# Layer normalisations of a two-layer model: ScalarE makes the high parts, VectorE the full values, on two PSUM banks in turn

## The chip, the cores and the metric

The kernel runs on one core of a Trainium2 chip. The metric is the device time of one execution in microseconds (us); lower is better. Before the change the median of three runs is 2249.2 us (2247.33 to 2249.74).

The engines are named as the profile names them: PE is TensorE's matmul, PEld its weight load, DVE is VectorE, ACT is ScalarE, POOL is GpSimd, SP is SyncE. "L876" is line 876 of the kernel before.

## The reference, cut to what matters

Four batches of 1024 rows with 256 features go through two layers. Each layer has two residual branches, and each branch starts with a layer normalisation that is scaled and shifted per batch:

```python
h = _layernorm(x, axis=-1) * (1 + ca) + sa
x = x + ga * _L0_attn_ref(h, ...)      # gated long convolution
h = _layernorm(x, axis=-1) * (1 + cb) + sb
x = x + gb * _L0_ffn_ref(h, ...)       # FFN with binarised weights, exact GELU
h = _layernorm(x, axis=-1) * (1 + ca) + sa
x = x + ga * _L1_attn_ref(h, ...)      # causal attention, 16 heads on 4 KV heads
h = _layernorm(x, axis=-1) * (1 + cb) + sb
x = x + gb * _L1_ffn_ref(h, ...)       # the two experts chosen per batch
```

## The kernel before, in words

Everything is float32. Where a product needs full precision, an operand is kept as two parts of the reduced type F32R: the high part is the value rounded to that type, the low part is the full value minus the high part. `hT[:, 0]` is the high and `hT[:, 1]` the low part of the transposed, normalised input of a branch. The matmuls that read `hT` (`split_mm` at L300 and `sign_mm` at L306) need both.

One batch is one turn of a hardware loop on every engine; the engines run the same stages and meet by semaphores. In order of time, a batch is: the convolution branch, the FFN, attention, the experts. There are four normalisations in a turn: LN_FFN, LN_ATT, LN_MOE and LN_NEXT (the convolution's, for the next batch). The first batch's own is made once ahead of the loop. Each is made in two halves of 512 rows (h = 0 and 1), and a half goes like this:

1. DVE `normed`: it ends the statistics, hands the variance to POOL, which returns `rstd` (L1140, 1.02 us), and writes four tiles of `hrow` (L867).
2. PE `normed`: for each of two feature tiles dt it transposes four tiles of `hrow` into one PSUM bank (L378).
3. ACT `normed`: for each dt it reads the bank twice with the same scale and bias. L672 writes the full value into `hfull`, L673 the rounded one into `hT[:, 0]`, and that counts `hT_done`.
4. DVE `h_low`: for each dt it waits for `hT_done` and writes `hT[:, 1] = hfull - hT[:, 0]` (L876), which counts `h_lo_done`. PE waits for it in `h_ready`, and ACT waits for it before it writes a ring slot of `hfull` again.

What stands around each half in DVE's program order matters, since each engine works strictly in its order:

- LN_FFN 0: `h_low` stands between `skip_and_gate(1)` and `add_to_x("out0", 1)`; PE makes `long_out(1)` meanwhile, and then the first half of the FFN.
- LN_FFN 1: PE turns it after five of the first half's eight FFN tiles. DVE does `hrow`, then splits four GELU tiles (L1059 and L1061), then `h_low`, then twelve more splits. PE waits for this `h_low` before the second half.
- LN_ATT 0: DVE does `add_to_x("ffn2", 1)` and then `h_low`; then PE projects tiles 0 to 3 (L300).
- LN_ATT 1: DVE does `hrow`, `rotate` of two tiles, `h_low`; then PE projects tiles 4 to 7.
- LN_MOE 0: PE turns it ahead of the last tile of the attention's output product (L610), and the router needs its low part.
- LN_MOE 1: `h_low` stands behind the split of the first expert's weights. Behind it DVE splits the second expert's and makes LN_NEXT's statistics.
- LN_NEXT: `h_low` for both halves stands behind both `hrow`; the next instruction on DVE is the first `add_to_x("moe2", 0)`.

PSUM has eight banks, taken in turn; `bk.take(..., until=...)` names the semaphore count that makes a bank free for PE again.

Of the kernel before, what the change touches and what calls it, by code (L numbers as in the profile page):

```python
# [85 lines left out]
def adaln_hyena_binffn_gqa_moe(nc, d, out, gate_scratch, kf_scratch, scratch):  # L86
    es = ExitStack()
    with es:
# [121 lines left out]
        def rotated(t):  # L210
# [12 lines left out]
                 "rstd_done", "hrow_done", "hT_done", "bias_added", "tap_made", "tap_done", "edge_done", "conv_done", "vx_done",  # L223
# [68 lines left out]
        def _(pe):  # L292
# [77 lines left out]
            def normed(k, h):  # L370

                for dt in range(ND):
                    b = bk.take(pe, ("ln", k, h, dt), until=(s["hT_done"], (k * NHALF + h) * ND + dt + 1))
                    for u in range(4):
                        t = 4 * h + u
                        if dt == 0:
                            pe.wait_ge(s["hrow_done"], k * NT + t + 1)
                        i = tr(ps[:, b, u * P:(u + 1) * P], hrow[:, t, dt * P:(dt + 1) * P], ident[:, :])  # L378
                    i.then_inc(ready[b], 1)
# [260 lines left out]
        def _(act):  # L640
# [23 lines left out]
            def normed(k, h, mod):  # L664

                for dt in range(ND):
                    n = (k * NHALF + h) * ND + dt
                    b = bk.wait(act, ("ln", k, h, dt))
                    if n >= 2:
                        act.wait_ge(s["h_lo_done"], n - 1)  # L670
                    args = {"bias": mod[:, 0, dt:dt + 1], "scale": mod[:, 1, dt:dt + 1]}
                    A(hfull[:, n % 2, :], ps[:, b, :], ACT.Identity, **args)  # L672
                    A(hT[:, 0, dt, h * HALF:(h + 1) * HALF], ps[:, b, :], ACT.Identity, **args)\  # L673
                        .then_inc(s["hT_done"], 1)
# [119 lines left out]
        def _(dve):  # L794
# [75 lines left out]
            def h_low(k, h):  # L870

                for dt in range(ND):
                    n = (k * NHALF + h) * ND + dt
                    cols = slice(h * HALF, (h + 1) * HALF)
                    dve.wait_ge(s["hT_done"], n + 1)
                    V.tensor_tensor(hT[:, 1, dt, cols], hfull[:, n % 2, :], hT[:, 0, dt, cols].bitcast(F32),  # L876
                                    ALU.subtract).then_inc(s["h_lo_done"], 1)

# [25 lines left out]
            for h in range(NHALF):  # L904
                h_low(0, h)
# [84 lines left out]
            with dve.Fori(0, B) as bi:  # L990
# [58 lines left out]
                h_low(LN_FFN, 0)  # L1049
                add_to_x("out0", 1, gates[:, 0, :], bias=1)  # L1050
                normed(LN_FFN, 1, x)
                for h in range(NHALF):
                    for n in range(NH1):
                        if (h, n) == (0, FFN_LOW):
                            h_low(LN_FFN, 1)
# [7 lines left out]
                for h in range(NHALF):  # L1063
                    add_to_x("ffn2", h, escale[:, 0, :], bias=2)
                    if h:
                        h_low(LN_ATT, 0)
                    normed(LN_ATT, h, x)
                rotate(0, range(2))
                h_low(LN_ATT, 1)
# [24 lines left out]
                h_low(LN_MOE, 0)  # L1094
# [8 lines left out]
                for k in range(TOPK):  # L1103
                    dve.wait_ge(s[f"w1_loaded{k}"], 16)
                    split([w1s[:, k, a, :, :] for a in range(2)], w1e[:, k, :, :], s["w1_split"])
                    if k == 0:
                        h_low(LN_MOE, 1)
# [7 lines left out]
                for h in range(NHALF):  # L1115
                    h_low(LN_NEXT, h)
# [291 lines left out]
```

## Time and profile before

| | |
|---|---|
| median of 3 runs | 2249.2 us |
| the profiled execution | 2249.1 us |
| its span in the profile | 2247.3 us |
| PE busy | 1951.0 us (87%) |
| DVE busy | 1338.3 us (60%) |
| ACT busy | 829.1 us (37%) |
| POOL busy | 508.1 us (23%) |
| granted TensorE clock, mean | 0.931 |

Busy shares are averages over stages with different limits. What a stage is worth is read from the stretch itself: which engine has no idle time in front of its instructions there, and whose wait ends last. In the timeline view a line is a start and a duration in us, the engine, the line of the kernel, the operation and its tiles, a count where equal instructions are merged, and in brackets the idle time of that engine before it with the releaser. Where no bracket stands, the engine had no idle time to speak of.

### The profile page before, as it was taken

What the parts mean: (1) busy time and instruction counts of PE and PEld (TensorE: products, weight loads), DVE (VectorE), ACT (ScalarE), POOL (GpSimd) and SP (SyncE); (2) the same over time, 40 slices, a digit from 0 to 9 for tenths busy, and PEclk for the clock granted to TensorE, in tenths of its full rate; (3) what the DMA queues carried; (4) which work ended last, traced back from release to release, by engine and by line L of the source; (5) the groups of instructions that cost most, each with busy time, mean ns of one, the idle gap of its engine ahead of it and who ended that gap; (6) DMA issues with size and microseconds to landing.
All of it is one profiled execution on the core that took longest, in us unless ns stands there. A gap on an engine that the chain in (4) does not pass through costs nothing.

```text
span 2247.3 us, 32490 instructions
## 1 busy us (share of the span) xinstructions
PE 1951.0 (87%) x11892; PEld 1739.9 (77%) x11892; DVE 1338.3 (60%) x3102; ACT 829.1 (37%) x1673; POOL 508.1 (23%) x991
## 2 busy tenths in 40 slices
PE   6868799999876789999976879999987688999997
PEld 4657699999755788999865769989976577999896
DVE  4598555553558755555358865555454985655535
ACT  1303444543321345445231334454422034444423
POOL 0051222121134221221016122212112421222101
PEclk8988899999988889999988889999998798999998
DMA  5400000000410000000050000000041000000005
GB/s 208 178 1 1 1 1 1 1 1 1 168 48 1 1 1 1 1 1 2 13 204 0 1 1 1 1 1 2 1 164 53 1 1 1 1 1 2 1 1 187
DMA packets 28522, 70.77 MB, mean 31 GB/s; under 512 B 4607, under 2 KB 19775, under 8 KB 24774
## 3 DMA queue, kind: packets, MB, share of 16 engines
q1 hardware_dynamic: 28358, 68.60, 8.3%
q8 instruction: 100, 1.64, 0.3%
q14 instruction: 64, 0.52, 0.1%
HBM read 58.35 MB, written 9.98 MB: 30 GB/s over the span
## 4 chain that ended last, share of the span: by engine, by line
PE 60%; DVE 20%; ACT 6%; issue 5%; DVEq 4%; DMA 2%; POOL 2%; POOLq 1%; SPq 1%; ACTq 0%
PE ps L454 20%; PE ps L300 8%; DVE ps L961 6%; PE ps L610 5%; PE ps L423 5%; PE ps L441 4%; PE ps L440 4%; PE ps L306 4%; PE ps L633 3%; PE ps L402 2%; ACT qhh L696 2%; DVE prod L1021 2%; DVE hrow L867 1%; DMA gate_scratch<-grow 1%; DVEq L1043 1%
## 5 line engine op out<-in xcount | busy, mean ns | idle before, releaser
L454 PEld LDWEIGHTS ps<-v,pT 128*128 128x128 f32 x4608 | 546.0, 192 | 12.6 <-ACT pT L713 1.9
L454 PE MATMUL ps<-v,pT 128*128 128x65 f32 x4608 | 538.4, 272 | 1.5 <-ACT pT L713 1.5
L713 ACT ACTIVATE pT<-ps 128x512 f32<-128x512 f32 (+3 forms) x768 | 332.7, 493 | 344.5 <-PE ps L441 332.7
L961 DVE CUSTOM_DVE_ANT_0 ps<-ps,mrow 128x128 f32<-128x128 f32 (+7 forms) x512 | 373.2, 784 | 39.5 <-PE ps L423 39.5
L1173 POOL TENSOR_SCALAR_AFFINE_SELECT pT<-pT 128x128 f32<-128x128 f32 x512 | 145.4, 292 | 928.7 <-ACT pT L713 922.9
L440 PE MATMUL ps<-qhh,khl 128*128 128x512 f32 (+3 forms) x768 | 275.8, 363 | 9.2 <-DMA q<-nmr 9.2
L441 PE MATMUL ps<-q,k 65*128 65x512 f32 (+3 forms) x768 | 261.9, 354 | 0.0
L423 PE MATMUL ps<-khl,qhh 128*128 128x512 f32 (+3 forms) x768 | 228.4, 379 | 36.9 <-DVE mx L961 14.8
L971 DVE RECIPROCAL den<-ps 128x4 f32<-128x4 f32 x128 | 23.4, 183 | 299.8 <-PE ps L454 299.8
L954 DVE TENSOR_TENSOR q<-ps,qhh 64x512 fp32r<-64x512 f32 x128 | 87.4, 683 | 186.6 <-ACT qhh L696 186.6
L672 ACT ACTIVATE hfull<-ps,modb 128x512 f32<-128x512 f32 x48 | 37.3, 776 | 434.4 <-PE ps L378 434.4
L423 PEld LDWEIGHTS ps<-khl,qhh 128*128 128x128 f32 x768 | 126.7, 194 | 71.0 <-DVE mx L961 39.1
L440 PEld LDWEIGHTS ps<-qhh,khl 128*128 128x128 f32 x768 | 149.6, 195 | 30.8 <-issue 10.4
L300 PE MATMUL ps<-wqkv,hT 128*128 128x384 f32 x768 | 147.4, 353 | 25.4 <-DVE hT L876 25.4
L300 PEld LDWEIGHTS ps<-wqkv,hT 128*128 128x128 f32 x768 | 141.4, 200 | 27.3 <-DVE hT L876 27.3
L441 PEld LDWEIGHTS ps<-q,k 65*128 65x128 f32 x768 | 149.7, 195 | 14.7
L696 ACT ACTIVATE qhh<-ps 64x512 fp32r<-64x512 f32 x256 | 151.0, 590 | 6.8 <-PE ps L402 2.3
L1140 POOL TENSOR_TENSOR rstd<-var,neghalf 128x4 f32<-128x4 f32 x34 | 34.5, 1014 | 453.7 <-DVE var L864 453.7
L610 PE MATMUL ps<-wo,oT 128*128 128x256 f32 x512 | 112.8, 380 | 0.0
L300 PE MATMUL ps<-hT,in_w 128*128 128x512 f32 x288 | 80.4, 445 | 36.9 <-issue 25.8
L610 PEld LDWEIGHTS ps<-wo,oT 128*128 128x128 f32 x512 | 96.3, 190 | 12.6
L300 PEld LDWEIGHTS ps<-hT,in_w 128*128 128x128 f32 x288 | 62.7, 221 | 53.7 <-issue 31.2
(162 smaller groups left out, 2854.4 us busy)
## 6 DMA issues: line engine op xcount, KB each, us to landing
sgn<-sgn_scratch SPq DMA_DIRECT2D x8, 1024.0 KB, 13.7
Kf<-kf_scratch SPq DMA_DIRECT2D x4, 2048.0 KB, 17.1
in_w<-in_w_scratch SPq DMA_DIRECT2D x4, 1536.0 KB, 10.7
x<-in_x SPq DMA_DIRECT2D x5, 1024.0 KB, 5.4
xn<-in_x SPq DMA_DIRECT2D x4, 1024.0 KB, 7.4
out<-x SPq DMA_DIRECT2D x4, 1024.0 KB, 5.0
wraw<-in_wmod SPq DMA_DIRECT2D x2, 1536.0 KB, 6.7
fwd<-in_fwd SPq DMA_DIRECT2D x5, 512.0 KB, 18.3
```

Of the source, the lines that this page charges most:

```text
L300: i = mm(o, lhs(a, q), rhs(c, q), start=n == 0, stop=n == len(pairs) - 1)
L306: i = mm(o, lhs(a, q), rhs(a, q), start=n == 0, stop=n == len(pairs) - 1)
L423: q = mm(ps[:, b + c // HALF, 0:e - c], qhh[:, r, i * P:(i + 1) * P], khl[:, g % 2, c:e], start=True, stop=True)
L440: mm(ps[:, b, 0:hi - lo], khl[:, g % 2, j * P:(j + 1) * P], qhh[:, r, lo:hi], start=True, stop=False)
L441: mm(ps[:, b, 0:hi - lo], k2[:, g % 2, j * P:(j + 1) * P], q2[:, r, lo:hi], start=False, stop=True)\
L454: q = mm(ps[:, b, (i % 4) * (HD + 1):(i % 4 + 1) * (HD + 1)], pT[:, slot, i * P - lo:(i + 1) * P - lo], v1[:, g % 2, j, :], start=j == 0, ...
L610: i = mm(ps[:, b, u * D:(u + 1) * D], oT[:, q, (t + u) * P:(t + u + 1) * P], wo[:, q, :], start=q == 0, stop=q == HEADS // 2 - 1)
L696: i = A(qhh[half:half + HD, u % QRING, h * HALF:(h + 1) * HALF], ps[0:HD, b, :], ACT.Copy)
L713: A(pT[:, n % PRING, 0:(c + 1) * HALF - lo], ps[:, b, 0:(c + 1) * HALF - lo], ACT.Exp, scale=SCALE)\
L954: V.tensor_tensor(q2[0:HD, u % QRING, cols], ps[0:HD, b, :], qhh[0:HD, u % QRING, cols].bitcast(F32), ALU.subtract).then_inc(s["q_lo_done" ...
L961: V.tensor_tensor_reduce(out=v, in0=v, in1=mrow[:, L - n:L], scale=1.0, scalar=-3e38, op0=ALU.add, op1=ALU.max, accum_out=mx[:, u % 2, i:i ...
L1173: G.affine_select(out=v, in_=v, compare_op=ALU.is_ge, fill=0.0, base=0, pattern=[[1, P]], channel_multiplier=-1).then_inc(s["masked_done"], 1)
```

## The change

ACT makes only the high parts: one instruction for each dt, in the order dt = 0, 1. DVE makes the full values itself out of the same PSUM banks with a multiply-add by per-partition scale and shift, in the order dt = 1, 0. Then, behind a drain, it makes the two low parts, and drains again. Each engine moves to the bank that the other has left only when the other is done with it: ACT waits for `full_done` before dt = 1, DVE for `hT_done` before dt = 0. The ring of `hfull` now goes by dt, and ACT no longer waits for `h_lo_done`. A bank is free for PE when its second reader is done. Nothing else is moved; `h_low` keeps its place in DVE's order.

```diff
             def normed(k, h):          # tensor engine
 
                 for dt in range(ND):
-                    b = bk.take(pe, ("ln", k, h, dt), until=(s["hT_done"], (k * NHALF + h) * ND + dt + 1))
+                    until = s["hT_done"] if dt else s["full_done"], ((k * NHALF + h) + 1) * ND
+                    b = bk.take(pe, ("ln", k, h, dt), until=until)
...
             def normed(k, h, mod):     # scalar engine
 
                 for dt in range(ND):
-                    n = (k * NHALF + h) * ND + dt
                     b = bk.wait(act, ("ln", k, h, dt))
-                    if n >= 2:
-                        act.wait_ge(s["h_lo_done"], n - 1)
-                    args = {"bias": mod[:, 0, dt:dt + 1], "scale": mod[:, 1, dt:dt + 1]}
-                    A(hfull[:, n % 2, :], ps[:, b, :], ACT.Identity, **args)
-                    A(hT[:, 0, dt, h * HALF:(h + 1) * HALF], ps[:, b, :], ACT.Identity, **args)\
-                        .then_inc(s["hT_done"], 1)
+                    if dt:
+                        act.wait_ge(s["full_done"], (k * NHALF + h) * ND + 1)
+                    A(hT[:, 0, dt, h * HALF:(h + 1) * HALF], ps[:, b, :], ACT.Identity,
+                      bias=mod[:, 0, dt:dt + 1], scale=mod[:, 1, dt:dt + 1]).then_inc(s["hT_done"], 1)
...
-            def h_low(k, h):
-
+            def h_low(k, h, mod):      # vector engine
+
+                m, cols = (k * NHALF + h) * ND, slice(h * HALF, (h + 1) * HALF)
+                for dt in (1, 0):
+                    b = bk.wait(dve, ("ln", k, h, dt))
+                    if dt == 0:
+                        dve.wait_ge(s["hT_done"], m + 1)
+                    V.tensor_scalar(hfull[:, dt, :], ps[:, b, :], mod[:, 1, dt:dt + 1], mod[:, 0, dt:dt + 1],
+                                    ALU.mult, ALU.add).then_inc(s["full_done"], 1)
+                dve.drain()
                 for dt in range(ND):
-                    n = (k * NHALF + h) * ND + dt
-                    cols = slice(h * HALF, (h + 1) * HALF)
-                    dve.wait_ge(s["hT_done"], n + 1)
-                    V.tensor_tensor(hT[:, 1, dt, cols], hfull[:, n % 2, :], hT[:, 0, dt, cols].bitcast(F32),
+                    dve.wait_ge(s["hT_done"], m + dt + 1)
+                    V.tensor_tensor(hT[:, 1, dt, cols], hfull[:, dt, :], hT[:, 0, dt, cols].bitcast(F32),
                                     ALU.subtract).then_inc(s["h_lo_done"], 1)
+                dve.drain()
```

The other lines of the diff pass the scale and shift of each normalisation to `h_low` and declare `full_done`.

## Rows read from the trace of the kernel before

**Rows 1.** Waits: who waited for whom, us in total, times, longest us.

```profile
PE ps L300 <- DVE hT L876: 25.4, 8, 3.2
PE ps L306 <- DVE hT L876: 16.5, 4, 4.1
```

**Rows 2.** ACT's groups by form: line, shapes, count, busy us, mean ns.

```profile
L673 ACT ACTIVATE hT<-ps,modb 128x512 fp32r<-128x512 f32 x48 | 37.3, 776 | 0.0
```

**Rows 3.** Timeline of DVE: prices of instructions that read PSUM, and a drain.

```profile
27.18 1.52 DVE L826 TENSOR_SCALAR ang<-ps,fb 64x512 f32<-64x512 f32 x2 [0.17 <-issue]
...
217.89 0.68 DVE L917 TENSOR_TENSOR tmp<-ps,escale 128x512 f32<-128x512 f32 x1
218.66 0.69 DVE L920 TENSOR_TENSOR x<-x,tmp 128x512 f32<-128x512 f32 x1
```

**Rows 4.** Timeline, first batch, LN_FFN 1.

```profile
190.82 1.29 DVE L876 TENSOR_TENSOR hT<-hfull,hT 128x512 fp32r<-128x512 f32 x2
...
192.17 10.32 PE L306 MATMUL ps<-hT,sgn 128*128 128x512 f32 x32 [4.14 <-DVE hT L876]
```

**Rows 5.** Timeline, first batch, LN_ATT 0.

```profile
220.26 0.69 DVE L876 TENSOR_TENSOR hT<-hfull,hT 128x512 fp32r<-128x512 f32 x1
...
221.13 0.69 DVE L876 TENSOR_TENSOR hT<-hfull,hT 128x512 fp32r<-128x512 f32 x1 [0.18 <-ACT hT L673]
221.88 5.68 PEld L300 LDWEIGHTS ps<-wqkv,hT 128*128 128x128 f32 x24 [3.40 <-DVE hT L876]
```

**Rows 6.** Timeline, LN_ATT 1, of the first batch and of the third.

```profile
227.72 1.03 PE L378 MATMUL ps<-ident,hrow 128*128 128x128 f32 x8
...
231.17 0.69 DVE L876 TENSOR_TENSOR hT<-hfull,hT 128x512 fp32r<-128x512 f32 x1 [0.65 <-ACT hT L673]
...
1308.76 0.69 DVE L876 TENSOR_TENSOR hT<-hfull,hT 128x512 fp32r<-128x512 f32 x1
...
1310.10 0.76 DVE L876 TENSOR_TENSOR hT<-hfull,hT 128x512 fp32r<-128x512 f32 x1 [0.65 <-ACT hT L673]
```

**Rows 7.** Timeline, LN_FFN 0, of the first batch and of the second.

```profile
173.33 1.28 DVE L876 TENSOR_TENSOR hT<-hfull,hT 128x512 fp32r<-128x512 f32 x2
...
176.60 0.69 DVE L917 TENSOR_TENSOR tmp<-ps,gates 128x512 f32<-128x512 f32 x1 [1.99 <-PE ps L516]
...
715.36 1.28 DVE L876 TENSOR_TENSOR hT<-hfull,hT 128x512 fp32r<-128x512 f32 x2
...
717.59 0.69 DVE L917 TENSOR_TENSOR tmp<-ps,gates 128x512 f32<-128x512 f32 x1 [0.95 <-PE ps L516]
```

**Rows 8.** Timeline, first batch, LN_MOE 0: the last low part, the router.

```profile
577.24 0.69 DVE L876 TENSOR_TENSOR hT<-hfull,hT 128x512 fp32r<-128x512 f32 x1 [0.65 <-ACT hT L673]
...
577.99 0.43 PE L300 MATMUL ps<-wr,hT 128*1 128x8 f32 x6
```

**Rows 9.** Timeline, first batch, LN_MOE 1.

```profile
586.75 2.21 PE L378 MATMUL ps<-ident,hrow 128*128 128x128 f32 x8 [4.77 <-DVE hrow L867]
...
590.95 0.69 DVE L876 TENSOR_TENSOR hT<-hfull,hT 128x512 fp32r<-128x512 f32 x1 [0.65 <-ACT hT L673]
```

**Rows 10.** Timeline, first batch, LN_NEXT and the first addition behind it.

```profile
604.95 4.03 DVE L876 TENSOR_TENSOR hT<-hfull,hT 128x512 fp32r<-128x512 f32 x3
605.08 1.33 PE L378 MATMUL ps<-ident,hrow 128*128 128x128 f32 x5 [0.94 <-DVE hrow L867]
...
612.39 0.69 DVE L917 TENSOR_TENSOR tmp<-ps,escale 128x512 f32<-128x512 f32 x1 [1.75 <-PE ps L633]
```

**Rows 11.** Timeline, ahead of the loop: the first batch's own normalisation.

```profile
84.92 1.29 DVE L876 TENSOR_TENSOR hT<-hfull,hT 128x512 fp32r<-128x512 f32 x2
...
88.52 0.69 DVE L876 TENSOR_TENSOR hT<-hfull,hT 128x512 fp32r<-128x512 f32 x1 [0.64 <-ACT hT L673]
```

**Rows 12.** Windows behind LN_ATT 0, second and third batch: clock third last.

```profile
761.60:763.60 2.00, 2.00 (x6) 2.00 (x7) 0.76 (x6) 0.00 (x0) 1.14 (x3) 0.50 0.00 0
1302.00:1304.00 2.00, 2.00 (x12) 2.00 (x12) 0.78 (x6) 0.00 (x0) 1.15 (x3) 1.00 0.00 0
```

More of the change, by code:

```diff
@@ L222, in adaln_hyena_binffn_gqa_moe @@
                  "mod_picked", "x_loaded", "x_next_loaded", "gates_loaded", "gates_mixed", "var_done",
-                 "rstd_done", "hrow_done", "hT_done", "bias_added", "tap_made", "tap_done", "edge_done", "conv_done", "vx_done",
+                 "rstd_done", "hrow_done", "hT_done", "full_done", "bias_added", "tap_made", "tap_done", "edge_done", "conv_done", "vx_done",
                  "vrow_done", "prod_done", "y_dve", "y_pool", "yv_done", "gelu_done", "g_lo_done", "h_lo_done",
@@ L904, in _ @@
             for h in range(NHALF):
-                h_low(0, h)
+                h_low(0, h, modn)
             part_ends(dve, "vector")
@@ L1048, in _ @@
                 skip_and_gate(1)
-                h_low(LN_FFN, 0)
+                h_low(LN_FFN, 0, modb[:, 0, 2:4])
                 add_to_x("out0", 1, gates[:, 0, :], bias=1)
@@ L1054, in _ @@
                         if (h, n) == (0, FFN_LOW):
-                            h_low(LN_FFN, 1)
+                            h_low(LN_FFN, 1, modb[:, 0, 2:4])
                         m = h * NH1 + n
@@ L1065, in _ @@
                     if h:
-                        h_low(LN_ATT, 0)
+                        h_low(LN_ATT, 0, modb[:, 1, 0:2])
                     normed(LN_ATT, h, x)
                 rotate(0, range(2))
-                h_low(LN_ATT, 1)
+                h_low(LN_ATT, 1, modb[:, 1, 0:2])
                 rotate(0, range(2, NT))
@@ L1093, in _ @@
                 normed(LN_MOE, 0, x)
-                h_low(LN_MOE, 0)
+                h_low(LN_MOE, 0, modb[:, 1, 2:4])
                 b = bk.wait(dve, ("router",))
@@ L1106, in _ @@
                     if k == 0:
-                        h_low(LN_MOE, 1)
+                        h_low(LN_MOE, 1, modb[:, 1, 2:4])
                 pick_first((bi + 1) % B)
@@ L1115, in _ @@
                 for h in range(NHALF):
-                    h_low(LN_NEXT, h)
+                    h_low(LN_NEXT, h, modn)
                 for h in range(NHALF):
```

## The prediction

> **What bounds the kernel now.** I read the waits first, since an average share says nothing of a stage. PE waits 25.4 us in eight waits and 16.5 us in four for the low parts that DVE writes at L876 [rows 1]. So three of the eight halves of a batch end in a wait of PE for `h_low`: LN_FFN 1, LN_ATT 0 and LN_ATT 1. The question at each half is what ended last there: ACT, which this change unloads by half, or DVE, which it loads. For that I read the timeline round each half and look for the bracket in front of DVE's L876. A bracket says that DVE stood still for ACT; none says that DVE was itself the last to arrive.
>
> At LN_FFN 1 both low parts run back to back, 1.29 us for the two with no bracket [rows 4]: DVE was busy with GELU splits, and ACT had long been done. At LN_ATT 0 the first has no bracket and the second one of 0.18 us [rows 5]. Only at LN_ATT 1 in the first batch (0.65 us), LN_MOE 0, LN_MOE 1 and ahead of the loop does DVE stand still for ACT [rows 6, 8, 9, 11]. The two halves with the longest waits of PE are therefore bound by the engine that gets more work.
>
> **The new half in DVE's time.** Removed: the `hfull` instruction of ACT, 0.776 us by the row of its twin [rows 2], twice in a half. Added on DVE: two multiply-adds from PSUM and two drains. The nearest row is the only tensor_scalar in the trace that reads PSUM with two per-partition scalars: a pair of them takes 1.52 us [rows 3]. It covers 64 partitions instead of 128, but the elements per partition are the same 512. A drain adds 0.09 us: the addition at 218.66 starts that long after the product of 217.89 has ended, 218.66 - 217.89 - 0.68 [rows 3]. Then come the two low parts, 1.29 us as before. So a half takes 1.52 + 0.09 + 1.29 = 2.90 us on DVE from its first instruction, where it took 1.29. The swap itself adds nothing when both engines are there: ACT's second high part starts about 0.9 us in and ends about 1.7 us in (0.776 us long), and its low part starts 2.2 us in. Lower bound of the pair: a product from PSUM takes 0.68 us [rows 3], as long as one low part, so a pair of them 1.29 like the low parts, 0.23 less. Upper bound: the two don't overlap at all, about 0.1 more. I take 1.52, the same operation.
>
> The Trainium skill (VectorE: DVE Perf Modes, section on the TRN2 errata) gives a VectorE instruction from PSUM to SBUF 120 cycles and one for each element at 0.96 GHz, which would be an estimate of 0.66 us for 512 elements. The trace differs for the form with two pointer scalars, where the row is longer. By the page each exposed half would be about 0.3 us cheaper and the total about 4 us lower.
>
> **Half by half.** "Start" is where DVE's first instruction of the half can begin.
> - LN_FFN 1, four times. DVE starts where it does now and takes 2.90 instead of 1.29: +1.61, all of it before the matmuls at 192.17 that waited 4.14 us [rows 4]. Queued behind it are twelve splits, which shift with it, and ACT's three GELUs behind the high part, needed only later. Sum 6.4.
> - LN_ATT 0, four times. Start 220.26, end 223.16 instead of 221.13 + 0.69 = 221.82 [rows 5]: +1.34, in front of PE's wait of 3.40 us. Sum 5.4.
> - LN_ATT 1. In the first two batches the second bank is ready at 227.72 + 1.03 = 228.75 and DVE is free, so the end is 231.75 instead of 231.86: -0.1. In the third DVE has no bracket at 1308.76 [rows 6]; end 1311.66 instead of 1310.86: +0.8, and the fourth batch looks the same. Sum 1.4.
> - LN_FFN 0. Behind it stands an addition that waits for PE. First batch: 173.33 + 2.90 + 0.09 = 176.32, cover until 176.60. Second: 715.36 + 2.99 = 718.35 against 717.59, so +0.76, for that chain runs through DVE to LN_FFN 1 [rows 7]. In the third and fourth PE's tiles come about as late as in the first, and I count nothing. Sum 0.8.
> - LN_MOE 0. The router's matmuls begin at 577.99 with no wait [rows 8]. The new low part would end near 577.8 instead of 577.93: nothing.
> - LN_MOE 1. The second bank is ready at 586.75 + 2.21 = 588.96; end about 591.96 instead of 591.64 [rows 9], plus the last drain: +0.4. Queued behind it is the whole of LN_NEXT, and PE waits for that `hrow` at 605.08 [rows 10], so it is exposed, but for one batch where a DMA ends last. Sum 1.2.
> - LN_NEXT. Four low parts become eight instructions, two times 2.99 us, with POOL's additions slowing the first ones as now (4.03 us for three [rows 10]). I get an end near 612.0, and the addition waits for PE until 612.39. Were it late, the additions behind it are paced by PE's four tiles and would catch up. Nothing.
> - Ahead of the loop, once: two halves from 84.92 are 5.9 us, end 90.8 instead of 89.2 [rows 11]: +1.6.
>
> Sum: 6.4 + 5.4 + 1.4 + 0.8 + 1.2 + 1.6 = 16.8 us. The profiled execution took 2249.1 us, 1.8 more than its span of 2247.3, and stands 0.1 below the median. The forecast is 2249.1 + 16.8 = 2265.9, rounded to 2266. ACT's 53 us of removed work (68 times 0.776) buy nothing where DVE is last; that is the core of the argument.
>
> **The rivals.**
> 1. PE's clock falls more often. PE's waits grow from 3.2 to 4.5 us at LN_ATT 0 and from 4.1 to 5.8 at LN_FFN 1. Behind the same wait the granted clock is 0.50 (1.2 GHz) in the second batch and 1.00 (2.4 GHz) in the third [rows 12]. PE makes 6 matmuls in 2 us at the one and 12 at the other. If the third and fourth batch fall too, some 3 us at half speed cost about 1.5 us each behind LN_ATT 0, partly taken back because DVE is then free earlier at LN_ATT 1, and some 0.5 us for each LN_FFN 1: +3 to +5, total 2270. The Trainium skill (TensorE: Matmul & The Clock Gate, the section on the clock gate) says the same: an idle array falls to half its clock and activity frees it.
> 2. The multiply-add is cheaper than its nearest row: a pair takes 1.29 instead of 1.52 us. The sum has 16 exposed halves (4 + 4 + 2 + 1 + 3 + 2), so 3.7 us less, total 2262.
> 3. Not slower. The mechanism is ACT as the bound of each half: its four instructions of 0.776 us become two, and DVE finds the bank ready and itself free. Then each half ends 0.1 us earlier, as at LN_ATT 1 in the first batch, and in all 34 halves that is 3 us: 2246, the same within what can be measured. It decides from the point where DVE has 1.6 us free ahead of `h_low`. The missing brackets at LN_FFN 1 and LN_ATT 0 speak against it; PE falling less often could help by a few us more but not by 17.
> 4. The change doesn't overlap as it says: ACT's second high part or DVE's second multiply-add is held up by the swap, for instance because each waits for the other's end and the hand-over costs 0.1 to 0.2 us more than counted. The low part has 0.5 us of room, so it costs at most 0.2 us for a half, total 2268.
>
> **How the numbers follow.** The forecast as summed, with its price for the multiply-add, has a chance of 0.5; rival 1 0.17; rival 2 0.17; rival 4 0.08; rival 3 0.08. About 0.2% (4.5 us) is what a measurement of this kernel can tell from no change. The base and rivals 1, 2 and 4 all lie over 2253.7. Rival 3 splits into 0.06 for the same and 0.02 for faster, and I add 0.02 for a sum that comes out below 4.5 us. The range goes from 2258 (the cheap multiply-add, and some exposed halves covered) to 2273 (the clock, and a bad LN_NEXT).
>
> **What would show each step.** In the changed kernel's trace, the wait of PE L306 for the low part should read about 5.7 us each and that of L300 behind LN_ATT 0 about 4.5; the multiply-adds a pair of 1.5 us; `hfull` no longer on ACT, whose busy time falls by 53 us, while DVE's rises by about 52. The addition at LN_NEXT should still wait for PE. I am wrong if the pair takes under 1 us, if DVE shows idle time in front of its multiply-adds at LN_FFN 1, or if the clock behind the two longer waits is higher than now.

## The result and the profile after

The changed kernel has a median of 2265.35 us in four runs (2261.18 to 2268.55), the kernel before 2249.47 us beside it (2247.33 to 2252.19, four runs). The ratio is 1.0069, with an interval of 1.0049 to 1.0089: slower by 16 us, or 0.7%. The forecast was 2266, the range 2258 to 2273. The profiled execution of the changed kernel is its fastest, 2261.18 us with a span of 2259.4, so its stages explain 12.1 us of span and not 16.

The page of the changed kernel, busy time of each engine and the slices of the granted clock:

```profile
PE 1948.5 (86%) x11892; PEld 1739.6 (77%) x11892; DVE 1383.8 (61%) x3170; ACT 786.7 (35%) x1605; POOL 505.0 (22%) x991
...
PEclk9989899999997899999988889999998788999998
```

ACT lost 42.4 us of busy time, DVE gained 45.5, and PE's own busy time fell by 2.5. So the time must be looked for in PE's waits. Waits of the changed kernel (us in total, times, longest us):

```profile
ACT hT L671 <- DVE hfull L875: 71.0, 34, 4.0
...
PE ps L300 <- DVE hT L880: 30.1, 8, 4.5
...
PE ps L306 <- DVE hT L880: 23.0, 4, 5.8
```

L875 is the new multiply-add, L880 the low part (L876 before), L671 ACT's high part. Against [rows 1] PE waits 6.5 us more in four waits and 4.7 us more in eight. ACT, which was to be relieved, now waits for DVE in all 34 halves.

Timeline of the changed kernel (start, duration, engine, line, operation, tiles, count, idle time before and its releaser), DVE ahead of the loop, answering to [rows 3, 11]:

```profile
85.86 1.52 DVE L875 TENSOR_SCALAR hfull<-ps,modn 128x512 f32<-128x512 f32 x2
...
87.48 1.29 DVE L880 TENSOR_TENSOR hT<-hfull,hT 128x512 fp32r<-128x512 f32 x2
```

LN_FFN 1, first batch, answering to [rows 4]:

```profile
193.94 1.52 DVE L875 TENSOR_SCALAR hfull<-ps,modb 128x512 f32<-128x512 f32 x2
195.14 0.78 ACT L671 ACTIVATE hT<-ps,modb 128x512 fp32r<-128x512 f32 x1 [3.99 <-DVE hfull L875]
195.56 1.29 DVE L880 TENSOR_TENSOR hT<-hfull,hT 128x512 fp32r<-128x512 f32 x2
...
196.91 1.65 PE L306 MATMUL ps<-hT,sgn 128*128 128x512 f32 x3 [5.76 <-DVE hT L880]
```

LN_ATT 0, first batch, answering to [rows 5]:

```profile
223.62 1.53 DVE L875 TENSOR_SCALAR hfull<-ps,modb 128x512 f32<-128x512 f32 x2
...
225.25 1.29 DVE L880 TENSOR_TENSOR hT<-hfull,hT 128x512 fp32r<-128x512 f32 x2
...
226.59 1.55 PEld L300 LDWEIGHTS ps<-wqkv,hT 128*128 128x128 f32 x7 [4.76 <-DVE hT L880]
```

No bracket stands in front of either multiply-add, and both banks were there. From the first DVE instruction to PE's start it is 196.91 - 193.94 = 2.97 us at LN_FFN 1 where it was 192.17 - 190.82 = 1.35 [rows 4]: +1.62, against 1.61 forecast. At LN_ATT 0 it is again 226.59 - 223.62 = 2.97, where it was 221.88 - 220.26 = 1.62 [rows 5]: +1.35, against 1.34.

### The profile page after: what moved, and what is told of

Same layout as the page of the kernel before. It is cut to its first block, busy times and chain, and to the rows that moved or that the text cites. A ratio compares the mean times of both kernels' runs of the same rounds, so it can differ in the third digit from the quotient of the medians.

```text
span 2259.4 us, 32568 instructions
## 1 busy us (share of the span) xinstructions
PE 1948.5 (86%) x11892; PEld 1739.6 (77%) x11892; DVE 1383.8 (61%) x3170; ACT 786.7 (35%) x1605; POOL 505.0 (22%) x991
## 4 chain that ended last, share of the span: by engine, by line
PE 59%; DVE 20%; DVEq 6%; ACT 5%; issue 4%; DMA 2%; POOL 2%; POOLq 0%; SPq 0%; ACTq 0%
PE ps L455 20%; PE ps L300 9%; DVE ps L966 6%; PE ps L611 5%; PE ps L424 4%; PE ps L442 4%; PE ps L441 4%; PE ps L306 3%; PE ps L634 3%; PE ps L403 2%; ACT qhh L694 2%; DVE prod L1026 2%; DMA gate_scratch<-grow 2%; DVEq L877 1%; DVEq L1048 1%
## 5 line engine op out<-in xcount | busy, mean ns | idle before, releaser
L671 ACT ACTIVATE hT<-ps,modb 128x512 fp32r<-128x512 f32 x48 | 37.3, 777 | 489.9 <-PE ps L379 444.8
L300 PE MATMUL ps<-wqkv,hT 128*128 128x384 f32 x768 | 152.7, 362 | 30.1 <-DVE hT L880 30.1
L300 PEld LDWEIGHTS ps<-wqkv,hT 128*128 128x128 f32 x768 | 146.6, 207 | 32.0 <-DVE hT L880 32.0
L300 PE MATMUL ps<-hT,in_w 128*128 128x512 f32 x288 | 79.9, 443 | 38.8 <-issue 25.8
L300 PEld LDWEIGHTS ps<-hT,in_w 128*128 128x128 f32 x288 | 62.3, 219 | 55.5 <-issue 32.9
```

Source lines behind the costliest of these rows:

```text
L300: i = mm(o, lhs(a, q), rhs(c, q), start=n == 0, stop=n == len(pairs) - 1)
```

## Where the time went, stage by stage

To compare two traces I took the same landmark of each stage in both (the start of PE's first matmul of it, or of DVE's first addition), formed the time from landmark to landmark, and summed over four batches. "New in two" and "old in two" are experiments 2 and 3, "no swap" is experiment 4. A row's label names the landmark at which the stage ends; so "LN_ATT 1's transposes" is the time in which PE projects tiles 0 to 3. All in us longer than the kernel before, each from one profiled execution ("again" is a second execution of the changed kernel, experiment 1):

| from the landmark before to | changed | again | new in two | old in two | no swap |
|---|---|---|---|---|---|
| start of the loop | 2.6 | 5.0 | 0.5 | 2.2 | 1.9 |
| convolution and the first FFN tiles, to LN_FFN 1's transposes | 2.7 | 3.3 | -0.2 | 2.8 | 0.9 |
| second half of the FFN (LN_FFN 1) | 6.5 | 6.5 | 6.5 | 0.0 | 6.5 |
| FFN's second product | 0.4 | 0.6 | 0.9 | 3.7 | 1.3 |
| projection of tiles 0 to 3 (LN_ATT 0) | 5.4 | 5.4 | 5.4 | 0.0 | 5.7 |
| LN_ATT 1's transposes | 5.1 | 5.5 | 5.6 | 3.1 | 5.7 |
| projection of tiles 4 to 7 (LN_ATT 1) | -1.5 | -1.5 | -0.9 | -1.5 | 0.3 |
| the heads, to the output product | -5.0 | -5.0 | 1.6 | 0.2 | 0.3 |
| router, first expert (LN_MOE 0 and 1) | 0.0 | 0.0 | 0.0 | 0.0 | 1.6 |
| second expert's product | -1.5 | -1.2 | -1.2 | 1.9 | 1.1 |
| last addition behind it (LN_NEXT) | -2.5 | -2.5 | -5.2 | -0.3 | -0.4 |
| sum | 12.2 | 16.0 | 13.0 | 12.1 | 24.9 |

The row with 6.5 is alike to 0.1 us in every kernel that has the new way there. The row with 5.4 is so too with the swap, and 5.7 without it. Both are zero in the kernel that has the old way. The others don't add up to simple prices: the heads give -5.0 in one program and +1.6 in another, though no edit touches them. Where I looked into them with windows, they carry the granted clock.

At LN_ATT 1 of the third batch, answering to [rows 6], the changed kernel's timeline and a window behind LN_ATT 0 (start:end, length, then busy us and count of PE, PEld, DVE, ACT, POOL; the clock is third last):

```profile
1317.75 1.03 PE L379 MATMUL ps<-ident,hrow 128*128 128x128 f32 x8
1318.83 1.53 DVE L875 TENSOR_SCALAR hfull<-ps,modb 128x512 f32<-128x512 f32 x2 [0.79 <-PE ps L379]
1320.45 1.29 DVE L880 TENSOR_TENSOR hT<-hfull,hT 128x512 fp32r<-128x512 f32 x2
...
1321.80 1.66 PE L300 MATMUL ps<-wqkv,hT 128*128 128x384 f32 x7 [3.01 <-DVE hT L880]
```

```profile
1311.30:1313.30 2.00, 2.00 (x6) 2.00 (x7) 0.74 (x6) 0.00 (x0) 1.11 (x3) 0.50 0.00 0
```

In the kernel before PE made 12 matmuls in such a window at 1.00 here [rows 12], now 6 at 0.50 (1.2 GHz), behind a wait that had grown from 3.2 to 4.5 us. This is what rival 1 forecast: in the third and fourth batch the projection of tiles 0 to 3 takes 6.5 us from start to start where it took 4.3. But DVE used these 2 us, stands idle in front of the multiply-add (0.79 us, where [rows 6] has no bracket), and 0.6 is given back. That the longer wait is what brought the clock down is not shown: in experiment 3 the wait is the old one of 3.2 us, and in the same two batches the same projection takes 5.8 us.

In the other direction, windows in the first attention head of the changed kernel and of the kernel before:

```profile
260.40:262.40 2.00, 2.00 (x13) 1.68 (x11) 0.00 (x0) 1.41 (x4) 0.71 (x3) 0.75 0.00 0
```

```profile
256.00:258.00 2.00, 2.00 (x11) 1.66 (x9) 0.00 (x0) 1.41 (x4) 0.69 (x3) 0.50 0.00 0
```

The same work at the same place of the program, and the clock rises earlier after the change: 1.25 us a batch, 5 us in all. Nothing that I changed is there; only the moment at which the work falls is other.

Two smaller places. At LN_FFN 0 the forecast put its whole term into the second batch, so that batch is the one to read: the kernel before, then the changed one, answering to [rows 7]:

```profile
715.49 3.72 PE L516 MATMUL ps<-out_w,x 128*128 128x256 f32 x16 [2.81 <-DVE x L987]
```

```profile
717.93 5.41 PE L517 MATMUL ps<-out_w,x 128*128 128x256 f32 x16 [2.81 <-DVE x L992]
...
719.41 1.29 DVE L880 TENSOR_TENSOR hT<-hfull,hT 128x512 fp32r<-128x512 f32 x2
...
721.02 0.69 DVE L922 TENSOR_TENSOR tmp<-ps,gates 128x512 f32<-128x512 f32 x1 [0.32 <-PE ps L517]
```

The addition behind `h_low` still waits for PE, so the new work is covered. The batch is longer because PE's sixteen matmuls take 5.41 us instead of 3.72. The same difference stands in the traces of experiments 2 and 7, where LN_FFN 0 goes the old way. So it is no price of this half.

LN_NEXT of the changed kernel, answering to [rows 10]:

```profile
613.65 1.29 DVE L880 TENSOR_TENSOR hT<-hfull,hT 128x512 fp32r<-128x512 f32 x2
615.11 0.69 DVE L922 TENSOR_TENSOR tmp<-ps,escale 128x512 f32<-128x512 f32 x1 [0.16 <-issue]
...
617.88 0.69 DVE L922 TENSOR_TENSOR tmp<-ps,escale 128x512 f32<-128x512 f32 x1 [1.29 <-PE ps L634]
```

I had forecast that the first addition would still wait for PE. It doesn't, but the next ones do (1.29 us): the late first one is caught up, and it costs nothing.

And a gap that I can't explain. The same DVE instruction of the convolution in the changed kernel and in the kernel before:

```profile
684.88 1.23 DVE L1026 TENSOR_TENSOR prod<-ps,Kf 128x1024 f32<-128x1024 f32 x1 [0.53 <-issue]
```

```profile
682.41 1.22 DVE L1021 TENSOR_TENSOR prod<-ps,Kf 128x1024 f32<-128x1024 f32 x1 [0.16 <-issue]
```

It has no releaser and costs 0.37 us in every batch (1.4 us in all, in the table's second row). Of the kernels below it is there in 1, 3, 6, 8, 9 and 12 and not in 2, 4, 5, 7, 10 and 11. These two groups are not arbitrary: the first are all the kernels that make LN_FFN 0, LN_NEXT and the others besides LN_FFN 1 and LN_ATT 0 the new way with the swap. So the gap comes with the change, outside the instructions that it edits, and may be counted as part of its price. Its cause stays open.

## The experiments

My theory: DVE is the last to arrive at LN_FFN 1 and LN_ATT 0, so a half costs what DVE's new instructions last, and ACT's relief buys nothing; the granted clock adds and takes away a few us. The rival: the price is all clock, or it is the swap.

### 1. The changed kernel once more

No edit.

> The changed kernel once more, for a second trace and more times. Theory: the profiled execution of the change (2261.2 us) lies below its median (2265.4) because of where PE's granted clock rose behind the attention's start, so another execution should read the same waits (PE L306 for the low part 5.8 us, L300 behind LN_ATT 0 4.5 us) but a longer stretch at clock 0.50, and the median should be 2249.5 + 16 = 2265.5, within 2. Rival: 2261 is the kernel's own time and the others were noise: then the median moves to 2261 to 2262.

Measured 2265.06 us (2263.2 to 2268.85, five runs), ratio 1.0066 (1.0052 to 1.0080). The result stands. This trace has a span of 2263.3. From the second batch on its stages agree with those of the first trace within 0.4 us; the 4 us more lie in the start (2.4) and the first batch (1.6). The slices of the clock:

```profile
PEclk7889899999997899999988889999998788999998
```

It begins with 7 where the page above has 9. The same sixteen matmuls of the setup, in the first trace of the changed kernel and in this one:

```profile
48.94 4.11 PE L345 MATMUL ps<-fwo,sine 64*128 64x256 f32 x16
```

```profile
48.55 7.19 PE L345 MATMUL ps<-fwo,sine 64*128 64x256 f32 x16
```

The window 48.9 to 50.9 us has a granted clock of 1.00 in the first and 0.50 in this one. So one and the same kernel starts its loop 2.4 us later in one execution than in another. The start carries an uncertainty of this size, and is no part of a comparison of stages.

### 2 and 3. The new way in two halves, and in all the others

A list says which half of which normalisation goes which way; the instructions are those of the kernel before or of the changed one.

```diff
+NEW_HALVES = ((0, 1), (1, 0))      # LN_FFN 1, LN_ATT 0; setup the old way
...
+        def new_way(k, h, bk):
+            return NEW_SETUP if bk is banks["setup"] else (k, h) in NEW_HALVES
...
+                for dt in (1, 0) if new else ():
```

> Starts from the kernel before; only LN_FFN 1 and LN_ATT 0, the two halves where DVE arrives last, are made the new way. Theory: they carry 4 x 1.61 + 4 x 1.35 = 11.8 us of the cost, so 2249.5 + 11.8 = 2261 (range 2258 to 2265 with the clock). Rival (the swap or the clock costs about the same in each of the 34 halves): 8 of 34 halves give 16 x 8 / 34 = 3.8, so 2253.

Measured 2262.18 us (2261.94 to 2264.83), ratio 1.0057 (1.0043 to 1.0070): as expected, and 9 us over the rival's 2253. Two halves of eight, eight of 34 in all, carry 12 us.

```diff
-NEW_HALVES = ((0, 1), (1, 0))
-NEW_SETUP = False
+NEW_HALVES = ((0, 0), (1, 1), (2, 0), (2, 1), (3, 0), (3, 1))
+NEW_SETUP = True
```

> Starts from the changed kernel; only LN_FFN 1 and LN_ATT 0 go back to the old way, the other 26 halves stay new. Theory: 16.5 - 11.8 = 4 to 5 us of cost remain (LN_ATT 1 in two batches, LN_FFN 0 in one, LN_MOE 1, ahead of the loop), so 2254 (2251 to 2257). Rival (cost even over the halves): 2249.5 + 16 x 26 / 34 = 2262.

Measured 2261.14 us (2259.81 to 2265.55), ratio 1.0056 (1.0042 to 1.0069). That is 11 us slower than before and not 4 to 5: the expectation missed, and the number is that of the rival (2262). The rival doesn't fit experiment 2, though, and together the two give 23 us where the whole change costs 15 to 16: the costs don't add up. The table's fourth column says where the rest is. LN_FFN 1 and LN_ATT 0 are at 0.0, but 3.7 us stand behind LN_FFN 1 and 3.1 behind LN_ATT 0, where the program is that of the kernel before. Windows behind LN_FFN 1 in the second batch, of this kernel and then of the kernel before, both behind the same wait of 4.1 us (the first two and the third two us; the window between reads 0.50 in both):

```profile
736.70:738.70 2.00, 2.00 (x5) 1.61 (x6) 1.85 (x4) 0.00 (x0) 0.00 (x0) 0.50 0.00 0
...
740.70:742.70 2.00, 2.00 (x6) 1.61 (x5) 1.85 (x5) 1.07 (x2) 0.00 (x0) 0.51 0.00 0
```

```profile
733.10:735.10 2.00, 2.00 (x7) 1.61 (x8) 1.85 (x4) 0.75 (x1) 0.00 (x0) 0.74 0.00 0
...
737.10:739.10 2.00, 2.00 (x9) 1.65 (x8) 1.85 (x5) 1.25 (x2) 0.00 (x0) 0.91 0.00 0
```

So an edit elsewhere, which only moves the work in time, made the clock rise later behind an unchanged wait, and 6.7 of the 12.1 us of its trace stand in these two stages. The clock is a term of the size of the change's own, in either direction. Experiments 7 to 10 take it out in the stages whose waits they fill.

### 4. Without the swap

Both engines take dt = 0 first; ACT goes ahead without waiting for DVE, and DVE follows it on each bank (cut; ACT's wait and the count that frees a bank change with it).

```diff
-                for dt in (1, 0):
+                for dt in range(ND):
                     b = bk.wait(dve, ("ln", k, h, dt))
-                    if dt == 0:
-                        dve.wait_ge(s["hT_done"], m + 1)
+                    dve.wait_ge(s["hT_done"], m + dt + 1)
```

> Changed kernel without the swap: ACT makes both high parts one after the other without waiting for DVE, DVE makes each full value behind the high part of the same bank, in the order 0, 1. Theory (DVE's own 2.90 us of work set the end, the hand-over costs nothing): within 2 us of the changed kernel, 2266; at LN_ATT 1 of two batches 0.3 us later each. Rival (the hand-over between the banks holds both engines up by 0.1 to 0.2 us in a half): 2 to 3 us faster than the changed kernel, 2263.

Measured 2274.79 us (2273.89 to 2276.2), ratio 1.0110 (1.0095 to 1.0126): 9.7 us over the changed kernel, and a miss. At LN_MOE 0 DVE does wait for ACT's high part now (this kernel's timeline):

```profile
579.47 1.53 DVE L872 TENSOR_SCALAR hfull<-ps,modb 128x512 f32<-128x512 f32 x2 [2.65 <-ACT hT L669]
```

But that is 0.35 us a batch there and 0.1 at LN_ATT 0. In the table the large differences to the changed kernel are the heads (5.3 us), the second expert (2.7), the additions behind it (2.2) and LN_ATT 1 (1.8). Whether this is the clock is experiment 10.

### 5. ACT's relief alone

This kernel leaves out the full values: nobody makes them, and `hfull` holds zeros. DVE's instructions are those of the kernel before.

```diff
                     b = bk.wait(act, ("ln", k, h, dt))
-                    if n >= 2:
-                        act.wait_ge(s["h_lo_done"], n - 1)
                     args = {"bias": mod[:, 0, dt:dt + 1], "scale": mod[:, 1, dt:dt + 1]}
-                    A(hfull[:, n % 2, :], ps[:, b, :], ACT.Identity, **args)
```

> Kernel before, but ACT makes only the high parts and nobody makes the full values (hfull is filled with zeros once, so the low parts are not the right ones): ACT's relief without DVE's new work. Theory: nothing at LN_FFN 1, where DVE is last; 0.26 us at each LN_ATT 0; 1.3 us at LN_ATT 1 in two batches and 0.8 in two; 1.3 at three or four LN_MOE 1; 1.4 ahead of the loop: 11 us in all, so 2239 (2234 to 2244 with the clock). Rival (ACT's relief is worth nothing anywhere): 2250.

Measured 2236.48 us (2233.51 to 2239.97), ratio 0.9944 (0.9929 to 0.9959): 13.5 us, as expected. Waits of this kernel:

```profile
PE ps L300 <- DVE hT L873: 21.2, 8, 2.9
PE ps L306 <- DVE hT L873: 16.5, 4, 4.1
DVE hT L873 <- ACT hT L670: 13.1, 14, 2.6
```

The wait in front of LN_FFN 1 is 16.5 us in four, to the tenth that of [rows 1]: there ACT's relief is worth nothing. That of L300 falls from 25.4 to 21.2. So the relief is worth 4 us at LN_ATT. By the landmarks of the table, 5.5 more lie behind the start of the second expert's product and 2.9 ahead of it. How much of these is clock was not separated. Between this kernel and the changed one are 2265.1 - 2236.5 = 28.6 us; that is not a price of DVE's work alone, since the clock moves between them too.

### 6. The multiply-add with constants

This kernel leaves out the scale and shift of the full values.

```diff
-                    V.tensor_scalar(hfull[:, dt, :], ps[:, b, :], mod[:, 1, dt:dt + 1], mod[:, 0, dt:dt + 1],
+                    V.tensor_scalar(hfull[:, dt, :], ps[:, b, :], 1.5, 0.5,
```

> Changed kernel with two constants in place of the per-partition scale and shift in DVE's multiply-add (so the full values are not the right ones). Measures the disputed price by itself. Theory (the two per-partition scalars are what makes it 0.80 us instead of 0.69): the pair falls from 1.52 to about 1.29 us, 16 exposed halves give 3.7, so 2265.1 - 3.7 = 2261.5. Rival (it is reading PSUM that costs 0.80): the pair stays 1.52 and the time 2265.

Measured 2257.74 us (2250.05 to 2263.47, twelve runs), ratio 1.0029 (1.0015 to 1.0042). The group of this kernel, then that of the changed one (count, busy us, mean ns of one, idle before):

```profile
L875 DVE TENSOR_SCALAR hfull<-ps 128x512 f32<-128x512 f32 x68 | 43.7, 683 | 14.2 <-PE ps L379 13.4
```

```profile
L875 DVE TENSOR_SCALAR hfull<-ps,modb 128x512 f32<-128x512 f32 x48 | 36.6, 804 | 12.9 <-PE ps L379 12.6
```

The instruction falls from 804 to 683 ns, the pair from 1.52 to 1.28 us. The Trainium skill (VectorE: DVE Perf Modes, section on the TRN2 errata) gives an estimate of 0.66 us; the form with constants (0.683 us) is near it and the one with two scalars from memory (0.804) is not, and the page names no price for those. At LN_FFN 1 and LN_ATT 0 the stages are 0.24 us shorter in each batch than in the changed kernel, which is the pair's difference. Sixteen exposed halves by 0.24 us are 3.8 us, and 7.3 were measured, with runs spread over 13 us: the remainder was not traced.

### 7 and 8. Both kernels with PE kept busy in its waits

Surplus matmuls into a bank that nobody reads fill PE's long waits: ahead of the second half of the FFN, in front of both LN_ATT projections, before and after the first maxima, and ahead of LN_MOE 1. In the changed kernel 32 and 24 of them stand at LN_FFN 1 and LN_ATT 0 instead of 22 and 16, since its waits are longer.

```diff
+            def keep_busy(n):
+                b = bk.take(pe, ("busy", n), until=(s["mod_picked"], 1), at=bk.at % 8)
+                for _ in range(n):
+                    i = mm(ps[:, b, 0:GW], wqkv[:, 0, 0, 0, 0:P], wqkv[:, 0, 1, 0, :], start=True, stop=True)
+                i.then_inc(ready[b], 1)
...
                 for h in range(NHALF):
+                    if h:
+                        keep_busy(22)
                     h_ready(LN_FFN, h)
...
                     normed(LN_ATT, h)
+                    keep_busy((16, 16)[h])
                     h_ready(LN_ATT, h)
...
+                keep_busy(15)
                 turn_maxima(0)
+                keep_busy(11)
...
+                keep_busy(24)
                 normed(LN_MOE, 1)
```

> Kernel before with surplus matmuls on PE (0.16 us each at full clock, their result read by nobody) in the waits in front of LN_FFN 1's and LN_ATT's low parts (22, 16, 16), in the two waits ahead of the first head (15, 11) and ahead of LN_MOE 1 (24). Theory: they fit into the waits and the clock no longer falls: 9.8 us back in the FFN's second half, 3 at LN_ATT 0, up to 6 at LN_ATT 1, up to 11 in the first head, so 2250 - 25 = 2225 (2217 to 2235). Rival (the surplus matmuls delay the work behind them, or the clock falls all the same): 2250 or more.

Measured 2223.7 us (2221.36 to 2226.48), ratio 0.9887 (0.9873 to 0.9902): as expected, 26 us faster than the kernel before, and faster than every other kernel here. By the landmarks 7.2 us come back behind LN_FFN 1, 3.0 behind LN_ATT 0, 6.2 behind LN_ATT 1 and 8.3 in the heads. Timeline of PE and one window of this kernel:

```profile
189.07 3.98 PE L531 MATMUL ps<-wqkv 128*128 128x384 f32 x22
193.35 7.59 PE L306 MATMUL ps<-hT,sgn 128*128 128x512 f32 x32 [0.30 <-DVE hT L889]
...
220.44 4.43 PE L300 MATMUL ps<-wqkv,hT 128*128 128x384 f32 x24 [0.46 <-DVE hT L889]
```

```profile
193.30:195.30 2.00, 1.95 (x8) 1.61 (x9) 1.85 (x4) 0.69 (x1) 0.00 (x0) 1.00 0.04 8
```

The 32 matmuls behind LN_FFN 1 took 10.32 us [rows 4] and take 7.59, at a granted clock of 1.00 (2.4 GHz): the wait is filled, and what stands behind it gains. The Trainium skill (TensorE: Matmul & The Clock Gate, the section on the clock gate) says that an idle array falls to half its clock and that activity releases it; the trace agrees, with 0.50 in the first two us behind the wait in the kernel before (first batch) and 1.00 behind the surplus matmuls here.

> Changed kernel with the same surplus matmuls (32, 24 and 16 in the longer waits). It separates DVE's work from the clock: with the clock held in both, theory expects the direct costs alone between this and e7: 6.5 (LN_FFN 1) + 5.4 (LN_ATT 0) + up to 3 (LN_ATT 1, 0.8 in each batch since PE is now fast in all) + 1.2 (LN_MOE 1) + 1.6 (ahead of the loop) = 16 to 18 us above e7. Rival (the clock makes up half or more of the change's cost): 8 us or less above e7.

Measured 2246.86 us (2243.51 to 2251.79, eleven runs), ratio 0.9986 (0.9977 to 0.9995). Timeline of PE, the same two places, and LN_ATT 1:

```profile
194.03 5.71 PE L532 MATMUL ps<-wqkv 128*128 128x384 f32 x32
199.97 7.54 PE L306 MATMUL ps<-hT,sgn 128*128 128x512 f32 x32 [0.22 <-DVE hT L893]
...
228.49 4.43 PE L300 MATMUL ps<-wqkv,hT 128*128 128x384 f32 x24 [0.56 <-DVE hT L893]
...
238.14 4.43 PE L300 MATMUL ps<-wqkv,hT 128*128 128x384 f32 x24 [1.10 <-DVE hT L893]
```

It is 23.2 us over experiment 7, the kernel before with its waits filled. The clock behind the low parts of LN_FFN 1 and LN_ATT 0 is 1.00 in all batches of both traces, and the two stages cost +6.5 and +5.8: no less than with the clock left to itself. So their price is DVE's work and not the clock behind PE's waits, and the rival that gave at most 8 us falls. With LN_ATT 1 at +2.9 (0.72 in each batch, where DVE has no bracket), the second expert's product at +1.1 and the setup at +1.7 it is 18.0 us. Of the 1.1 about 0.5 is clock: in the first batch the last five transposes of LN_NEXT take 1.33 us where they took 0.81.

The other 5 us of the medians are not settled. The two traces differ by 30.5 us, since they are the slowest of eleven executions and the fastest of four. Beside the 18.0 they have 3.0 at the start of the loop, 1.4 of the unexplained gap, 1.3 elsewhere in the convolution, 2.5 in the heads and 4.3 up to the first addition of the second expert. At the second expert no wait is filled, and the clock is not level there. The second two us of the second expert's product in the second batch, experiment 7 and then this one:

```profile
1134.80:1136.80 2.00, 2.00 (x10) 1.70 (x10) 1.03 (x3) 1.49 (x3) 0.00 (x0) 0.92 0.05 18
```

```profile
1150.20:1152.20 2.00, 2.00 (x6) 1.55 (x6) 1.85 (x3) 0.68 (x1) 0.00 (x0) 0.50 0.06 23
```

### 9. As experiment 3, with PE kept busy

The surplus matmuls are those of experiment 7.

```diff
+NEW_HALVES = ((0, 0), (1, 1), (2, 0), (2, 1), (3, 0), (3, 1))
+NEW_SETUP = True
```

> The kernel of e3 (new way everywhere but at LN_FFN 1 and LN_ATT 0) with the surplus matmuls of e7. e3 cost 11 us where 4 to 5 were expected; its trace puts the rest into PE's clock. Theory (clock): with the clock held the remaining halves cost their direct price, 2.9 (LN_ATT 1) + 1.6 ahead of the loop + 1 to 2 (LN_MOE 1) = 6 us above e7's 2223.7, so 2230, within 3. Rival (the 26 other halves have a direct cost that the sum missed): 11 us or more above e7, 2235 or more.

Measured 2234.26 us (2233.37 to 2238.87), ratio 0.9928 (0.9915 to 0.9940): 10.6 us over experiment 7. That is above my 6 (within 3) and just under the rival's 11, so the expectation missed. By the landmarks the halves themselves take what was expected: 1.7 ahead of the loop, 2.6 at LN_ATT 1, 1.8 up to the second expert's product, 6.1 us in all. The unexplained gap adds 1.4. The rest is at places where none of these halves ends last. This trace is the slowest of its five and 17.6 us longer than that of experiment 7: 3.2 of them stand at the start of the loop, 1.2 elsewhere in the convolution, 2.4 in the heads and 3.3 up to the second expert's first addition. Beside the gap, a direct cost of the halves that the sum missed is not seen.

### 10. As experiment 4, with PE kept busy

The surplus matmuls are those of experiment 8.

```diff
-                for dt in (1, 0):
+                for dt in range(ND):
```

> The kernel of e4 (no swap) with the surplus matmuls of e8. e4 was 9.7 us over the changed kernel. Theory: the swap saves directly where DVE is at the bank before ACT has left it (0.45 us at each LN_ATT 1, 0.36 at each LN_MOE 0, 0.07 at each LN_ATT 0, some at LN_MOE 1), 4 to 5 us, the other half being the clock; so 2246.9 + 5 = 2252. Rival (all of it is direct): 2246.9 + 9.7 = 2256.6.

Measured 2247.05 us (2238.15 to 2252.33, twelve runs), ratio 0.9975 (0.9961 to 0.9989), the same as experiment 8 within some 3 us, which is what the intervals of the two leave open. The theory's 2252 and the rival's 2256.6 both missed. By the landmarks, taking the swap out costs 0.4 us a batch at LN_ATT 0 and 0.35 at LN_MOE 0, 3.0 in all, and as much comes back elsewhere, 1.4 of it the unexplained gap, which isn't there without the swap. So the swap has no worth that can be measured here, and most of the 9.7 us of experiment 4 are not its price. The table has them in stages without an edit; that they are clock fits, but was not read window by window.

### 11 and 12. LN_FFN 1's low parts two tiles earlier

If DVE is the bound at LN_FFN 1, its `h_low` could stand behind two splits instead of four.

```diff
-FFN_LOW = 4
+FFN_LOW = 2
...
-                        keep_busy(22)
+                        keep_busy(13)
```

> e7's kernel, and h_low of LN_FFN 1 stands behind two GELU splits instead of four (13 surplus matmuls there). PE can start the FFN's second half 1.3 us earlier in a batch; the fourteen splits behind it then end 0.4 us after PE's second tile instead of ahead of it. Expected 2223.7 - 4 x 0.9 = 2220. Rival (DVE's splits set the end of the stage, so their order is worth nothing): 2223.7.

Measured 2232.5 us (2230.88 to 2235.12), ratio 0.9921 (0.9908 to 0.9935): 8.8 us slower than experiment 7, and a miss. The first half of the expectation holds: PE starts the second half 1.34 us earlier in each batch. But from there to LN_ATT 0 it is 2.2 us longer, 0.9 more than was gained (+8.8 and -5.4 in four). The remaining 5 us are at places behind it, +3.1 of them in the projection of tiles 0 to 3, where PE now waits 1.8 us and its clock fell again in two batches of four. Timeline of this kernel at the end of the FFN's splits:

```profile
207.05 0.69 DVE L1074 TENSOR_TENSOR gT<-gfull,gT 128x512 fp32r<-128x512 f32 x1 [0.44 <-issue]
207.66 0.68 DVE L930 TENSOR_TENSOR tmp<-ps,escale 128x512 f32<-128x512 f32 x1
207.89 6.35 PE L306 MATMUL ps<-sgn,gT 128*128 128x256 f32 x51 [0.70 <-DVE gT L1074]
...
209.87 0.67 DVE L930 TENSOR_TENSOR tmp<-ps,escale 128x512 f32<-128x512 f32 x1
```

PE waits for the last split now (0.70 us), and DVE's additions have no idle time in front: fourteen splits and the first addition had been left to DVE behind `h_low`, and they are now what ends last. I had counted the splits and left out the addition.

```diff
-FFN_LOW = 4
+FFN_LOW = 2
...
-                        keep_busy(32)
+                        keep_busy(18)
```

> e8's kernel with the same move (18 surplus matmuls). In the new way DVE needs only the bank and not ACT's two passes, so PE's start moves by 2.2 us, of which 0.4 are lost behind it: 2246.9 - 4 x 1.8 = 2240. If the place of h_low could hide the new work, this would come down to e11's 2220; theory says no, since DVE has no idle time there at all.

Measured 2249.53 us (2245.88 to 2252.21, twelve runs), ratio 0.9994 (0.9985 to 1.0003): 2.7 us over experiment 8, a miss in the same way. The second half starts 2.2 us earlier in each batch (-8.85 in four), and LN_ATT 0 takes it all back (+8.8). DVE is the bound on either side of this half, and moving the half two splits ahead does not help.

## Why the prediction was right

- LN_FFN 1: forecast 6.4, measured 6.5, of which all is wait of PE. The wait reads 5.76 us (forecast 5.7). Experiment 3 is the counter-test: the old way there, and the stage is at 0.0.
- LN_ATT 0: forecast 5.4, measured 5.4; the wait reads 4.5 to 4.8 (forecast 4.5).
- LN_ATT 1: forecast 1.4, measured 5.1 - 1.5 = 3.6. The term is mis-sized, and in the third and fourth batch its mechanism was another. DVE's 0.8 was not paid there, for DVE stood idle (0.79 us); PE's clock in the projection before it cost 2.2 a batch, less 0.6 that DVE was free earlier. That is the clock fall of rival 1, but experiment 3 has 1.6 of the 2.2 without the longer wait. With the waits filled DVE's part is 0.72 in all four batches (experiment 8): the -0.1 of the first two holds only as long as PE is slow. The forecast's end of 231.75 also holds 0.1 us without a source; DVE starts 0.05 us behind the bank (1318.83 - 1317.75 - 1.03).
- LN_FFN 0: forecast 0.8, in the second batch. The step failed: the addition still waits 0.32 us for PE there, so the half costs nothing that can be read. The batch is longer by more than that, but by the clock of PE's sixteen matmuls, also where this half goes the old way.
- LN_MOE 0: forecast 0, measured -0.2.
- LN_MOE 1: forecast +0.4 for a batch; the first instruction behind the half came 3.28 us behind PE's start where it had been 2.83, +0.45. But the sum of the stage does not show it (0.0 up to the first expert, -1.5 behind), because the clock stood higher at the following transposes. With the waits filled the stage is 1.1 longer, part of it clock, and DVE's next instruction only 0.17 later. So the 1.2 is not confirmed.
- LN_NEXT: forecast 0. The step as told failed, the first addition did not wait for PE (0.16 us of issue for 1.75), but the next did, as the fall-back sentence had it. DVE was not later than forecast; PE's first tile was earlier, by its clock. The last addition, paced by PE, comes 2.5 us earlier behind the start of the product, summed over four batches; experiment 2, with the old way there, gains 5.2 in the same row.
- Ahead of the loop: forecast 1.6, measured 1.69 from the statistics' end to the loop's start. It is 0.0 in experiment 2, which has the old way there. The start itself differs by 2.4 us between two executions of one kernel.
- ACT's relief: forecast 53 us of ACT's busy time, measured 42.4. Two such instructions back to back start 0.67 us apart and last 0.78, so one less saves less than its duration. It was of no use at LN_FFN 1, as experiment 5 shows to the tenth. DVE's busy time rose by 45.5 and not 52: the new pairs took the 52, but the 68 low parts fell from 54.1 to 46.7.
- The multiply-add: a pair forecast 1.52 from a row on 64 partitions, measured 1.52 to 1.53 on 128. Rival 2 (1.29) is out; experiment 6 shows that it would have needed constants. (The prediction's estimate of 0.66 us for one instruction makes a pair 0.20 us cheaper and the total 3.2, not 0.3 and 4.)
- Rival 3, ACT as the bound: out, by the missing brackets in front of L875 at LN_FFN 1 and LN_ATT 0, and by ACT's 34 waits for DVE. Rival 4, a costly swap: out, since the multiply-adds follow each other without a gap (start to start 0.72 us in the pair of 1.52); experiment 10 finds no worth in the swap either way, within 3 us.
- One sign of being wrong did come up in part: behind LN_FFN 1 in the first batch the clock rose earlier than before, and the second half takes 8.8 us there for 10.2. In the other three batches it takes 0.5 to 0.7 us longer.

In the first trace the direct terms are 6.5 + 5.4 + 1.7 = 13.6 us, against 13.4 forecast for these three. The other 3.4 us of the forecast (LN_FFN 0, LN_ATT 1, LN_MOE 1) did not come as told. In their place stand 3.6 at LN_ATT 1, 1.4 for the unexplained gap, 1.3 more in the convolution, 0.4 in the FFN's second product and 0.9 at the start, and from the sum the heads and the second expert take 5.0 + 1.5 + 2.5 = 9.0. That makes 12.2. The medians differ by 16, and the second trace, of 16.0, has its 4 us more in the start and the first batch. So the mechanism is right and shown for the terms that carry the forecast. That the total came within 1 us of it is partly luck: the clock, which I had as a one-sided rival of +3 to +5, acts with both signs, and the sum of what it gave and took happened to be near the terms that failed.

## What to carry to other kernels

Read at each stage which engine has no idle time in front of its instructions; work moved off an idle engine onto that one costs nearly its full duration there, less what that engine had waited before (1.62 and 1.35 us here for 1.61 of new work). The average share (37% against 60%) says nothing. When two versions differ by less than a per cent, part of it may be clock: compare stage by stage, and if a stage without an edit has moved, fill PE's longest waits with surplus matmuls in both and compare again. This filling alone gained more (26 us) than any shift of work between engines did here.

## What the runs showed of the hardware

- The clock behind a wait is no function of the wait alone. Behind the same 4.1 us three windows in a row show 0.50, 0.50, 0.51 in one program and 0.74, 0.50, 0.91 in another; behind 3.2 us it is 0.50 in one batch and 1.00 in the next [rows 12]. A stage that no edit touches moved by up to 1.6 us a batch. Why the rise falls where it does was not settled; that it hangs on the moment at which the work arrives is only argued.
- 104 surplus matmuls a batch cost nothing at LN_FFN 1, where the second half starts as before to 0.01 us, and 0.12 us a batch at LN_ATT 0. The mean granted clock rose from 0.931 to 0.964 in the profiled executions.
- A VectorE multiply-add of 512 elements from PSUM takes 804 ns with two scalars from memory and 683 ns with two constants. A pair of the former takes 1.52 us, 0.72 from start to start, on 64 partitions as on 128.
- One VectorE instruction of the convolution had 0.53 us of issue ahead of it instead of 0.16 in all the kernels with the new, swapped way at LN_FFN 0 and LN_NEXT, and in no other. No run tells what does it.
